# Two products with a matrix of ones in the middle stage: plain fp32 against two rounded passes

## The reference, cut to what matters

```python
x = _layernorm(x + _L0_gnn_ref(x, adj, L0_gnn_bias), axis=-1)
x = _layernorm(x + _L1_gnn_ref(x, adj, W_lang, W_grav, W_V, W_O, gate_logit, log_sigma), axis=-1)
x = _layernorm(x + _L2_gnn_ref(x, adj, L2_gnn_bias), axis=-1)
x = _layernorm(x + _L3_gnn_ref(x, adj, adj, L3_gnn_bias), axis=-1)

# layer 1, per batch:
zn = z_l / max(norm(z_l), EPS)                 # z_l = h W_lang^T,  z_g = h W_grav^T
A_l = max(zn zn^T, 0) * not_eye
d2 = max(sq + sq^T - 2 z_g z_g^T, 0)           # sq = sum(z_g * z_g)
A_g = exp(-d2 / (2 sigma^2)) * not_eye
K = w_l * rows_sum_to_one(A_l * mask) + (1 - w_l) * rows_sum_to_one(A_g * mask)
out = (K v) W_O^T
```

## Time and profile before

| | |
|---|---|
| median of 3 runs | 1785.61 us (1785.38 to 1788.62) |
| the profiled execution: its time, its span | 1781.9 us, 1779.8 us |
| busy share of the span: PE / PEld / DVE / ACT / POOL | 88% / 71% / 72% / 47% / 31% |
| L986, product with `negones`, 128x512, plain fp32 | 32 matmul records (two for each of 16 products), 594 ns each |
| L992, product with `ones`, 128x512, plain fp32 | 32 matmul records, 594 ns each |
| r_l on POOL (L1255) | 16 times, 1022 ns each |
| sq_lo on POOL (L1250) | 64 times, 1295 ns each |

### The profile page before, as it was taken

One profiled execution on the slowest core, in us unless ns is written; L12 is line 12 of the kernel. 1 busy time (PEld: TensorE's weight loads), 2 busy tenths in 40 slices (PEclk: granted clock), 3 DMA queues, 4 the chain that ended last, 5 costly groups with the idle time before them and its releaser, 6 DMA issues. The chain is left out here.

```text
span 1779.8 us, 27351 instructions
## 1 busy us (share of the span) xinstructions
PE 1557.4 (88%) x7776; PEld 1268.6 (71%) x7776; DVE 1286.9 (72%) x3046; ACT 828.6 (47%) x1381; POOL 548.3 (31%) x749
## 2 busy tenths in 40 slices
PE   7899470599999999999999999998599791799997
PEld 4678330478888888888888888876488691577775
DVE  5798799347766677666776667765477699599997
ACT  7775220134344443444434444343333591377775
POOL 5652020012123221232212322122100000599997
PEclk9999685799999999999999999999699895799998
DMA  5320200101001110011100111000442000244442
GB/s 210 106 72 1 94 0 0 47 25 42 24 30 47 47 41 23 30 47 47 41 22 31 47 47 41 18 12 25 171 143 95 0 0 0 71 144 146 145 143 106
DMA packets 57580, 106.14 MB, mean 60 GB/s; under 512 B 5888, under 2 KB 6016, under 8 KB 57536
## 3 DMA queue, kind: packets, MB, share of 16 engines
q1 hardware_dynamic: 57536, 105.60, 17.7%
HBM read 71.90 MB, written 33.69 MB: 59 GB/s over the span
## 5 line engine op out<-in xcount | busy, mean ns | idle before, releaser
L773 POOL TENSOR_TENSOR rs_a<-ve_a,neghalf 128x1 f32<-128x1 f32 x64 | 34.6, 541 | 495.4 <-DVE nm_a L767 495.4
L232 PE MATMUL acc<-xn_lo,xn_hi 128*128 128x512 f32 (+1 forms) x640 | 145.4, 358 | 5.0 <-DVE xn_lo L203 4.8
L198 ACT ACTIVATE xn_hi<-xn 128x512 fp32r<-128x512 f32 x128 | 80.6, 630 | 117.1 <-DVE xn L191 117.0
L232 PEld LDWEIGHTS acc<-xn_lo,xn_hi 128*128 128x128 f32 x640 | 102.3, 192 | 19.2 <-DVE xn_lo L203 10.4
L1566 PE MATMUL l_ps<-an_hi,xw_hi 128*128 128x512 f32 x256 | 105.5, 412 | 9.8 <-POOL xw_lo L1627 8.4
L223 PEld LDWEIGHTS acc<-xn_hi 128*128 128x128 f32 x512 | 95.6, 192 | 24.3 <-ACT xn_hi L198 7.7
L923 PE MATMUL l_ps<-an_hi,xw_hi 128*128 128x512 f32 x256 | 103.2, 403 | 6.5 <-DVE xw_lo L1263 6.3
L564 DVE MATCH_REPLACE8 work<-best,work 128x520 f32<-128x520 f32 x160 | 107.7, 685 | 0.0
L329 POOL TENSOR_TENSOR sq_lo<-sq,sq_hi 128x512 fp32r<-128x512 f32 x64 | 87.3, 1380 | 61.2 <-ACT sq_hi L296 61.0
L203 DVE TENSOR_TENSOR xn_lo<-xn,xn_hi 128x512 fp32r<-128x512 f32 x128 | 105.8, 827 | 0.4 <-ACT xn_hi L198 0.2
L923 PE MATMUL l_ps<-an_hi,xw_lo 128*128 128x512 f32 x256 | 101.3, 396 | 0.0
(11 more groups left out here) (239 smaller groups left out, 4869.5 us busy)
## 6 DMA issues: line engine op xcount, KB each, us to landing
xr<-in_x SPq DMA_DIRECT2D x32, 512.0 KB, 3.5
xin<-in_x SPq DMA_DIRECT2D x64, 256.0 KB, 2.6
between<-xo SPq DMA_DIRECT2D x64, 256.0 KB, 2.0
xres<-between SPq DMA_DIRECT2D x32, 512.0 KB, 3.7
xin<-between SPq DMA_DIRECT2D x64, 256.0 KB, 2.7
out<-xo SPq DMA_DIRECT2D x64, 256.0 KB, 2.0
raw_lang<-in_L_gnn_W_lang SPq DMA_DIRECT2D x1, 1024.0 KB, 5.5
raw_grav<-in_L_gnn_W_grav SPq DMA_DIRECT2D x1, 1024.0 KB, 7.9
```

The source lines that it names most:

```text
L198: self.nc.scalar.activation(self.hi[:, i % 4, :], self.xn[:, i % 4, :], ACT.Copy).then_inc(self.hi_ready, 1)
L232: mm = self.nc.tensor.matmul(out, h[:, c * P:(c + 1) * P], l[:, a:b], start=False, stop=False, skip_group_check=True)
```

## The change

The two products with ones, `m_g_turned`'s last matmul and `r_rows`, are plain fp32 before. After, each is two matmuls with fp32r operands, the rounded part and the rest, against a constant matrix in fp32r.

- `prod[:, :, 1, :]` gets a rounded copy on ScalarE (`diagonal_hi`, after norm_a(3) and ahead of v_hi(1)) and a rest on GpSimd (after root_a(3) and ahead of `r_l`). The product moves on TensorE from the end of `m_g_turned` to a new step `diagonals_off`, behind hturn(1) and ahead of r_rows.
- `r_l` is split on VectorE: r_hi, r_lo, and two products with the identity in place of one.
- On VectorE `distances` moves from ahead of ht_lo(0) to behind v_lo(2).
- `sq2`, the buffer between ScalarE's square and GpSimd's `sq_lo`, has 2 places in place of 4 for the batches of a group, and `square(i)` waits until `sq_lo` of two batches earlier is done.

```diff
@@ gnn_layer_pair
-        dg_r = sb("dg_r", [P, GRP, P])
+        r_hi, r_lo = sb("r_hi", [P, GRP], F32R), sb("r_lo", [P, GRP])
+        dg = [sb(f"dg_{p}", [P, GRP, P], F32R) for p in ("hi", "lo")]
+        pr = [sb(f"pr_{p}", [P, GRP, P], F32R) for p in ("hi", "lo")]
-        sq = sb("sq2", [P, GRP, N])
+        sq = sb("sq2", [P, 2, N])
@@ tensor
-                    nc.tensor.matmul(tr[1][:], s.negones[:], prod[:, :, 1, :],
-                                     start=False, stop=True, skip_group_check=True).then_inc(mg_t, 1)
+                def diagonals_off():
+                    pe.wait_ge(pr_lo_ok, g + 1)
+                    for n, part in enumerate(pr):
+                        mm = nc.tensor.matmul(tr[1][:], s.negones_r[:], part[:].rearrange("p i n -> p (i n)"),
+                                              start=False, stop=(n == 1), skip_group_check=True)
+                    mm.then_inc(mg_t, 1)
                 def r_rows():
                     pe.wait_ge(dgr_ok, g + 1)
-                    nc.tensor.matmul(mp[0][:], s.ones[:], dg_r[:].rearrange("p i n -> p (i n)"),
-                                     start=True, stop=True).then_inc(r_row, 1)
+                    for n, part in enumerate(dg):
+                        mm = nc.tensor.matmul(mp[0][:], s.ones_r[:], part[:].rearrange("p i n -> p (i n)"),
+                                              start=(n == 0), stop=(n == 1))
+                    mm.then_inc(r_row, 1)
@@ scalar
+                def diagonal_hi():
+                    act.wait_ge(prod_ok, g + 1)
+                    copy(pr[0][:], prod[:, :, 1, :]).then_inc(pr_hi_ok, 1)
                 def square(i):
                     act.wait_ge(xo_ok, GRP * gp + i + 1)
-                    nc.scalar.activation(sq[:, i, :], xo[:, i, :], ACT.Square).then_inc(sq_ok, 1)
+                    act.wait_ge(sq_lo_ok, GRP * gp + i + 1)      # the counter starts at 2
+                    nc.scalar.activation(sq[:, i % 2, :], xo[:, i, :], ACT.Square).then_inc(sq_ok, 1)
@@ gpsimd
                 root_a(3)
                 if g is not None:
+                    pool.wait_ge(pr_hi_ok, g + 1)
+                    nc.gpsimd.tensor_tensor(pr[1][:], prod[:, :, 1, :], pr[0][:].bitcast(F32),
+                                            ALU.subtract).then_inc(pr_lo_ok, 1)
                     pool.wait_ge(q_ok, g + 1)
@@ vector
                 def diag_r():
                     dve.wait_ge(r_ok, g + 1)
-                    nc.vector.tensor_tensor(dg_r[:], over(s.ident[:], GRP), along(r_l[:], P), ALU.mult).then_inc(dgr_ok, 1)
+                    nc.vector.tensor_copy(r_hi[:], r_l[:]).then_inc(rs_ok, 1)
+                    dve.wait_ge(rs_ok, 2 * g + 1)
+                    nc.vector.tensor_tensor(r_lo[:], r_l[:], r_hi[:].bitcast(F32), ALU.subtract).then_inc(rs_ok, 1)
+                    nc.vector.tensor_tensor(dg[0][:], over(s.ident[:], GRP), along(r_hi[:].bitcast(F32), P), ALU.mult)
+                    dve.wait_ge(rs_ok, 2 * g + 2)
+                    nc.vector.tensor_tensor(dg[1][:], over(s.ident[:], GRP), along(r_lo[:], P), ALU.mult).then_inc(dgr_ok, 1)
```

More of the change, by code:

```diff
@@ L80, in constants @@
     sb, _, sem = scope(nc, ctx)
-    s.ident, s.ones, s.negones = sb("ident", [P, P]), sb("ones", [P, P]), sb("negones", [P, P])
+    s.ident, s.ones = sb("ident", [P, P]), sb("ones", [P, P])
+    s.ones_r, s.negones_r = sb("ones_r", [P, P], F32R), sb("negones_r", [P, P], F32R)
     s.zeros_r, s.pick, s.sel = sb("zeros_r", [P, N], F32R), sb("pick", [P, 2 * P], F32R), sb("sel", [P, HALF], F32R)
@@ L95, in fill @@
                                 base=0, pattern=[[-1, P]], channel_multiplier=1).then_inc(lined, 1)
-        nc.gpsimd.memset(s.negones[:], -1.0)
+        nc.gpsimd.memset(s.ones_r[:].bitcast(F32), 1.0)
+        nc.gpsimd.memset(s.negones_r[:].bitcast(F32), -1.0)
         nc.gpsimd.memset(s.neghalf[:], -0.5)
@@ L832, in gnn_layer_pair @@
         sq_hi_ok, sq_lo_ok = sem("sq_hi_ok"), sem("sq_lo_ok")
-        cf_ok, sg_ok = sem("cf_ok"), sem("sg_ok")
+        cf_ok, sg_ok, pr_hi_ok, pr_lo_ok, rs_ok = (sem(n) for n in ("cf_ok", "sg_ok", "pr_hi_ok", "pr_lo_ok", "rs_ok"))
         n2_made, n2_out, n2_stored = sem("n2_made"), sem("n2_out"), sem("n2_stored")
@@ L1011, in squares @@
                 def squares(half):
-                    pe.wait_ge(sq_lo_ok, GRP * gp + 2 * half + 2)
+                    pe.wait_ge(sq_lo_ok, 2 + GRP * gp + 2 * half + 2)
                     for i in (2 * half, 2 * half + 1):
@@ L1070, in turn @@
                 if B:
+                    diagonals_off()
                     r_rows()
@@ L1136, in square @@
                     act.wait_ge(xo_ok, GRP * gp + i + 1)
-                    nc.scalar.activation(sq[:, i, :], xo[:, i, :], ACT.Square).then_inc(sq_ok, 1)
+                    act.wait_ge(sq_lo_ok, GRP * gp + i + 1)
+                    nc.scalar.activation(sq[:, i % 2, :], xo[:, i, :], ACT.Square).then_inc(sq_ok, 1)
                     act.wait_ge(sq_ok, GRP * gp + i + 1)
-                    copy(sq_hi[:, i, :], sq[:, i, :]).then_inc(sq_hi_ok, 1)
+                    copy(sq_hi[:, i, :], sq[:, i % 2, :]).then_inc(sq_hi_ok, 1)
                 def sums_out():
@@ L1186, in turn @@
                 if B:
+                    diagonal_hi()
+                if B:
                     v_hi(1)
@@ L1205, in _ @@
             act.sem_inc(v_made, GRP)
+            act.sem_inc(sq_lo_ok, 2)
             act.sem_inc(n2_out, 1)
@@ L1249, in turn @@
                         pool.wait_ge(sq_hi_ok, GRP * gp + i + 1)
-                        nc.gpsimd.tensor_tensor(sq_lo[:, i, :], sq[:, i, :], sq_hi[:, i, :].bitcast(F32),
+                        nc.gpsimd.tensor_tensor(sq_lo[:, i, :], sq[:, i % 2, :], sq_hi[:, i, :].bitcast(F32),
                                                 ALU.subtract).then_inc(sq_lo_ok, 1)
@@ L1445, in turn @@
                     metric_l()
-                    distances()
                 if A:
@@ L1450, in turn @@
                     v_lo(2)
+                    distances()
                     kernel_l()
```

## The result

The changed kernel takes 1795.41 us (median of 5 runs, 1794.21 to 1797.21) against 1785.38 for the kernel before on the same chip (1782.30 to 1788.62): ratio 1.0056, 95% interval 1.0041 to 1.0071. It is 10 us slower; the forecast was 1794.6 us in a range of 1787 to 1800.

What follows compares the result with a forecast made beforehand. TensorE, busy 667.65 of 667.79 us in the middle stage, was taken as the bound. Losing 11.5 us, keeping 2.4 and losing 0.3 + 0.2 + 0.2 gave 9.8, rounded to +9: 1794.6 us, range 1787 to 1800.

Steps and rivals of the forecast that it cites:

- What the passes give: TensorE's two products with ones, split into fp32r passes, take 0.80 us less a turn (1.73 to 0.93).
- The first wait: End of a turn: xw(0) on TensorE waits for ht_lo(2), 0.28 us later; 0.17 us a turn kept.
- the start out of a wait: A TensorE matmul starting after a wait, as xw(0), takes 0.11 us more to its successor.
- The covers of 0.52 and 0.32: VectorE's idle times before v_lo(2), 0.52 us, and v_lo(3), 0.32 us, absorb part of the delay.
- The second wait: Smaller sq2: l0(3) on TensorE waits 0.71 us, plus 0.11 restart, so 0.82 us a turn lost.
- The sum: Whole program: 11.5 us lost, 2.4 kept, 0.3 + 0.2 + 0.2 lost at the edges, so 9.8 us slower.
- the rounding down to 9: Total of 9.8 us taken as +9, since some steps started 0.05 us ahead of their predecessor's end.
- passes are all that counts: Rival: neither new wait costs TensorE time, 12.7 us less the edges are kept, 1774 us; 4%.
- The ring's wait: Rival: the wait from the smaller sq2 is hidden, end of turn as worked out, 1784 us; 9%.
- The granted clock: Rival: new TensorE waits drop the clock to 1.2 GHz, costing some 40 us, 1836 us; 1%.
- TensorE itself has no wait in between: Within a turn, before xw(0), TensorE meets no new wait; ht_lo(1) has 0.2 us to spare for hturn(3).

Runs made afterwards that it cites:

- e3: Changed kernel with square(2) and square(3) moved on ScalarE to behind y_hi(3), ring of two and its wait kept: 1784.06 us, ratio 0.9995.
- e5: e3 plus kernel_g moved on VectorE from between ht_lo(1) and v_lo(3) to behind ht_lo(3): 1773.51 us, ratio 0.9942.
- e1: Changed kernel with three places in sq2 instead of two, only square(3) waiting, for sq_lo(0): 1783.10 us, ratio 0.9994.
- e2: Kernel before with only the two-place sq2 and its wait, products with ones left plain fp32: 1795.67 us, ratio 1.0064.
- e8: e3 plus r_l put ahead of pr_lo on GpSimd: 1791.78 us, ratio 1.0042.
- e10: e8 plus pr_lo on GpSimd waiting until r_hi is made: 1792.39 us, ratio 1.0056.
- e4: e3 with the split of r_l undone, so one dg_r and r_rows one plain fp32 product: 1781.20 us, ratio 0.9989.
- e6: e5 with the split of r_l undone, r_rows one plain fp32 product: 1778.24 us, ratio 0.9967.
- e9: e8 with r_hi written by a tensor_tensor in place of a tensor_copy: 1793.14 us, ratio 1.0058.
- e12: e5 with kernel_g back at its old place in the turn of group 15 only: 1774.07 us, ratio 0.9944.
- e7: Changed kernel with kernel_g moved behind ht_lo(3), squares left ahead of xw_hi(3): 1786.82 us, ratio 1.0010.

## Why the prediction was right

- *What the passes give.* hturn(2), which stands behind all four passes on TensorE, starts 10.21 us behind prod in the changed kernel and in e3, and 11.00 before: 0.79 us of TensorE's time saved; forecast 0.80. e5 kept 0.76.
- *The first wait.* Forecast: ht_lo(2) 0.28 later, xw(0) 0.28 earlier, 0.11 for the start out of a wait, 0.17 kept. Measured: 0.36 later, 0.20 earlier, 0.11 (xw(0) to yprod 0.92), and e1 and e3 keep 0.1 a turn. The term that was mis-sized is r_l: I had it 0.4 us later because pr_lo stands ahead of it on GpSimd; it is 0.58 later (3.34 behind prod against 2.76), because q_l on VectorE is held up by pr_lo as well. It comes in 13 turns, not the 14 of my sum. The covers of 0.52 and 0.32 that I named are gone in the timeline after: v_lo(2) and v_lo(3) have no idle time ahead of them.
- *The second wait.* Forecast 0.71 and 0.11, in 14 turns; measured, in 14 turns, 0.76 to 0.80 for l0(3) behind l0(2) (11.43 us in the turn shown and 11.47 in the median turn, against 10.67) and 0.11 (0.34 to its second matmul in place of 0.233). e2 has it alone at 0.94 a turn, e3 shows that it is the queue behind the wait. The trace of before gave each link of this chain, also why GpSimd is late: its sq_lo stand behind root_a(2).
- *The sum.* 0.84 a turn in place of 0.65. Of the 0.19 more, 0.07 is the first wait (0.10 kept, not 0.17) and some 0.12 the second (0.94 in e2, not 0.82). In the middle stage 12.0 us in place of 9.8; the rounding down to 9, for steps that start ahead of their predecessor's end, went the wrong way. 1.3 of the 12.0 lie in the first turn, and the last one is 0.25 shorter, not longer. The median moved 10.0. That it lies within 1 us of the forecast is in part luck: the stage alone is 3 us off, and the interval of the ratio leaves 7 to 13 us.
- *The rivals.* That passes are all that counts (1774 us) is what e5 reached, with two waits taken away. The ring's wait was not hidden. The granted clock stayed at 1.00 through both new waits, whose delays are 0.6 and 0.8 us.
- *Missed.* "TensorE itself has no wait in between" held with ht_lo(1), but I looked for nothing that could slow VectorE's instructions down themselves. By the rows this, r_l 0.58 us later and not 0.4, puts ht_lo(2) later than forecast; no run takes that delay away by itself (e8 to e10 only move it to another instruction).

## What to carry to other kernels

When a buffer is made smaller, look at what is queued behind the instruction that now needs a free place: here a ring of two places cost 12 us with the squares ahead of xw_hi(3) and nothing with them behind y_hi(3). A cheaper operation on the full engine is worth its price only up to the slack of the engine that it will then wait for, and an edit's value can change its sign with that (by turns, e4 and e6). Before a subtraction is put on GpSimd, look for what runs on VectorE in the same microsecond.

## What the runs showed of the hardware that was not expected

- A GpSimd subtraction of 128x512 with its inputs in SBUF (1.27 to 1.29 us) held up these VectorE instructions, which read only SBUF, when it had started first, in all 16 turns of the changed kernel (q_l), of e8 and of e9, and in 14 of 16 of e10: tensor_scalar 128x4 0.749 us in place of 0.169, copy 128x4 1.247 in place of 0.172, tensor_tensor 128x4 1.243, tensor_tensor 128x512 1.80 in place of 0.68. The hold-up does not show as idle time but as a longer instruction, and it hits the one that starts second (e10). Not every VectorE instruction is hit: mnn, a tensor_reduce that reads only SBUF, ran beside pr_lo for 0.51 us in all 16 turns of the changed kernel and took 1.220 us, as before (1.221), with pr_lo at 1.27; and xw_lo, with one input in PSUM, lay beside a sq_lo for its whole length in 14 turns there and took 0.69 us, its usual time. The Trainium skill, "SBUF — State Buffer", section "Who interferes with whom", says that copies, casts and tensor_scalar in their two-port modes contend with GpSimd, and a tensor_tensor with both inputs in SBUF with a GpSimd instruction that reads SBUF, and that the one issued first has the shared ports for its whole length. By that rule e9 had to fail; the traces agree.
- The first matmul of l0(3) out of its wait costs 0.11 us more to its successor (0.34 in place of 0.233 for 512 columns), xw(0) out of its wait 0.11 (0.92 in place of 0.81), and a start of xw(0) that was just in time 0.09 (e4).
- The length of TensorE's pauses did not by itself decide whether the granted clock fell. Behind pauses of 0.52 and 2.56 us, six matmuls apart, it was at 0.50 for about 3 us in e5 and e12 and stayed at 1.00 in e7; behind 0.53 and 1.69 it fell in e4 and stayed before; behind 1.25 and 1.33, in the first turn, it fell in e9 and stayed in e8 and e10. Each fall of this kind cost about 1.5 us.
